# The attention mask of a 192-step transformer pipeline: from a TensorE matmul to a ScalarE copy into PSUM, with two results moved to other banks

## What is computed

```python
qkv = x @ Wqkv                       # 16 heads of 64
q, k = l2norm(q) * qs, l2norm(k) * ksc   # then rotary
sim = einsum('bhwie,bhwje->bhwij', bq, bk2) * 8.0
sim = where(mask, -finfo.max, sim)   # windows of 32, own and previous
out = einsum('bhwij,bhwje->bhwie', softmax(sim), bv2)
x = out.reshape(b, n, 1024) @ Wo + x
```

## Time and profile before

| | us |
|---|---|
| median of 3 runs | 3785.27 |
| lowest, highest run | 3783.42, 3791.43 |
| the profiled execution | 3787.83 |
| its span | 3786.0 |

### The profile page before, as it was taken

How to read it: one execution, slowest core, us unless ns; L and a number is a source line. 1 busy time by engine, 2 the same in 40 slices (tenths; PEclk the granted TensorE clock), 3 DMA queues, 4 the chain that set the end, 5 groups by cost and what they waited for, 6 DMA issues and landing times.

```text
span 3786.0 us, 101581 instructions
## 1 busy us (share of the span) xinstructions
PE 3558.4 (94%) x42643; PEld 2250.6 (59%) x42643; DVE 3058.2 (81%) x5670; ACT 2037.8 (54%) x3871; POOL 2086.7 (55%) x1217
## 2 busy tenths in 40 slices
PE   8999699999999999999999999999999999999997
PEld 4555366666665666666665666666656666566664
DVE  3443698888898888888888898888888888888884
ACT  2222356565565565565655655656556556556553
POOL 0000376666566666666665666666666666666662
PEclk9999899999999999999999999999999999999998
DMA  2000000000001000001000001000001000000000
GB/s 66 1 1 1 7 10 12 28 10 10 9 14 32 10 10 7 10 16 29 10 10 10 7 16 32 10 7 10 10 15 31 10 10 7 14 12 16 10 10 12
DMA packets 62283, 52.55 MB, mean 14 GB/s; under 512 B 11526, under 2 KB 59396, under 8 KB 61828
## 3 DMA queue, kind: packets, MB, share of 16 engines
q1 hardware_dynamic: 61828, 46.05, 4.6%
HBM read 43.93 MB, written 2.10 MB: 12 GB/s over the span
## 4 chain that ended last, share of the span: by engine, by line
PE 62%; DVE 19%; issue 11%; POOL 5%; ACT 2%; DVEq 0%; DMA 0%; SPq 0%; POOLq 0%; ACTq 0%
PE ps L502 16%; PE ps L597 12%; PE ps L657 7%; PE ps L469 6%; PE ps L509 6%; DVE sinp L848 4%; DVE mx L938 3%; PE ps L643 3%; PE ps L551 3%; DVE pT L921 3%; PE ps L485 3%; PE ps L537 3%; POOL cosp L424 2%; POOL cosp L414 2%; DVE ss L854 2%
## 5 line engine op out<-in xcount | busy, mean ns | idle before, releaser
L414 POOL TENSOR_TENSOR cosp<-cosp,rr 128x1024 f32<-128x1024 f32 x384 | 722.5, 1902 | 823.1 <-DVE rr L65 823.0
L424 POOL TENSOR_TENSOR cosp<-cosp,sinp 128x1024 f32<-128x1024 f32 x384 | 904.7, 2368 | 96.1 <-DVE sinp L848 95.5
L502 PE MATMUL ps<-w_qk,xs 128*128 128x512 f32 x1536 | 814.9, 656 | 19.8 <-ACT sq L709 14.2
L597 PEld LDWEIGHTS ps<-px,w_vo 128*128 128x128 f32 x6144 | 729.5, 197 | 155.2 <-issue 118.7
L597 PE MATMUL ps<-px,w_vo 128*128 128x128 f32 x6144 | 739.6, 280 | 22.9 <-issue 18.4
L709 ACT ACTIVATE sq<-ps 128x1024 f32<-128x1024 f32 x384 | 393.1, 1024 | 571.3 <-DVE sinp L848 571.3
L845 DVE TENSOR_TENSOR cosp<-ps,tab 128x1024 f32<-128x1024 f32 x384 | 469.6, 1223 | 267.6 <-PE ps L502 267.4
L749 ACT COPY px<-ps 128x512 f32<-128x512 f32 x768 | 398.8, 598 | 431.0 <-PE ps L657 428.2
L657 PE MATMUL ps<-pT,xtm 32*128 32x512 f32 x3072 | 539.6, 629 | 88.3 <-DVE hh L869 74.7
L502 PEld LDWEIGHTS ps<-w_qk,xs 128*128 128x128 f32 x1536 | 279.9, 203 | 403.5 <-issue 401.8
L854 DVE TENSOR_REDUCE ss<-sq 128x16 f32<-128x1024 f32 x384 | 455.6, 1187 | 60.9 <-ACT sq L709 60.5
(11 more groups left out here) (101 smaller groups left out, 4094.2 us busy)
## 6 DMA issues: line engine op xcount, KB each, us to landing
tab<-in_tab SPq DMA_DIRECT2D x96, 128.0 KB, 2.0
qks<-in_scales SPq DMA_DIRECT2D x96, 128.0 KB, 3.2
w_qk<-in_L_ffn_Wqkv SPq DMA_DIRECT2D x12, 512.0 KB, 6.9
w_v<-in_wv_t SPq DMA_DIRECT2D x6, 512.0 KB, 8.7
w_o<-in_L_ffn_Wo SPq DMA_DIRECT2D x6, 512.0 KB, 9.1
x<-in_L_attn_x SPq DMA_DIRECT2D x16, 128.0 KB, 3.4
out<-w_v SPq DMA_DIRECT2D x16, 128.0 KB, 2.4
w<-in_L_ffn_W SPq DMA_DIRECT2D x6, 341.0 KB
```

The source lines that it names most:

```text
L414: eng.tensor_tensor(v, v, rr[:, B % 2, HEADS * i:HEADS * i + HEADS].unsqueeze(2).to_broadcast([P, HEADS, DH]), ALU.mult).then_inc(rot_read ...
L424: eng.tensor_tensor(cosp[:, A % 2, i, :], cosp[:, A % 2, i, :], sinp[:, i, :], ALU.add).then_inc(rot_added, 1)
L502: t = eng.matmul(ps[:, u, :], xs[:, n % ROUND, :], w_qk[:, n // TILES % 2, i, 512 * u:512 * u + 512], start=True, stop=True)
L597: t = eng.matmul(S0, w_vo[:, i // HP, i % HP, :], px[:, i, :], start=i == 0, stop=i == HEADS - 1)
```

## The change

- The mask is no longer written by TensorE, except for the first tile. In each step ScalarE copies the bf16 mask table into S (both banks, 128x1024) between its `xtm` and `qT` copies; it waits there for `centered` of the tile before and signals `mask_written`, for which the scores wait. The scores are added to what the copy left.
- The output projection goes to `Y`, the start of G(3) (bank 7), and the transposed tokens go to `X`, the start of G(0) (bank 4). The wait for `centered` ahead of the output projection goes.
- G(3) and G(0) are also the banks of the turned keys and of two of the Wv-Wo products. So the waits for `y_added` and `xt_evac` of the same step now stand ahead of `turn(B, 1)`, and in the layer step ahead of L608 too (L609 in the new numbering).

```diff
-        S0 = ps[:, 2, 0:P]
-        S1 = ps[:, 3, 0:P]
         G = lambda k: ps[:, 4 + k, :]
+        Y = G(3)[:, 0:P]
+        X = G(0)[:, 0:P]
@@ TensorE, step
-                if tile(C):
-                    eng.wait_ge(centered, C + 1)
                 if tile(E):
                     eng.wait_ge(px_evac, 4 * (E + 1))
...
-                        t = eng.matmul(S0, w_vo[:, i // HP, i % HP, :], px[:, i, :], start=i == 0, stop=i == HEADS - 1)
+                        t = eng.matmul(Y, w_vo[:, i // HP, i % HP, :], px[:, i, :], start=i == 0, stop=i == HEADS - 1)
...
-                    eng.transpose(S1, xs[:, C % ROUND, :], ident[:, :]).then_inc(xt_done, 1)
+                    eng.transpose(X, xs[:, C % ROUND, :], ident[:, :]).then_inc(xt_done, 1)
                 L = layer_of(s)
                 if L is not None:
                     eng.wait_ge(wv_in, 16 * (L + 1))
                     eng.wait_ge(wo_in, 16 * (L + 1))
+                    after(eng, y_added, E + 1)
+                    eng.wait_ge(xt_evac, C + 1)
...
                     project(A, 1)
+                if tile(E):
+                    eng.wait_ge(y_added, E + 1)
+                if tile(C):
+                    eng.wait_ge(xt_evac, C + 1)
                 if tile(B):
                     eng.wait_ge(rot_ready, 2 * B + 2)
                     turn(B, 1, K_BANKS)
...
                 if tile(B):
-                    if tile(E):
-                        eng.wait_ge(y_added, E + 1)
-                    after(eng, xt_evac, B)
-                    w = window(B)
-                    for h2 in range(2):
-                        eng.matmul(ps[:, 2 + h2, :].rearrange("p (h k) -> p h k", k=DH), ident_bf[:, :],
-                                   mask[:, DH * w:DH * w + DH].unsqueeze(1).to_broadcast([P, HP, DH]), start=True, stop=False, skip_group_check=True)
+                    if B == 0:
+                        for h2 in range(2):
+                            eng.matmul(ps[:, 2 + h2, :].rearrange("p (h k) -> p h k", k=DH), ident_bf[:, :],
+                                       mask[:, 0:DH].unsqueeze(1).to_broadcast([P, HP, DH]), start=True, stop=False, skip_group_check=True)
+                    after(eng, mask_written, B)
                     eng.wait_ge(turn_evac, 4 * B + 4)
@@ ScalarE, step
-                    eng.copy(xtm[:, C % NG, C % ROUND // 2, :], S1).then_inc(xt_evac, 1)
+                    eng.copy(xtm[:, C % NG, C % ROUND // 2, :], X).then_inc(xt_evac, 1)
+                if tile(B) and B:
+                    w = window(B)
+                    eng.wait_ge(centered, B)
+                    eng.copy(S, mask[:, DH * w:DH * w + DH].unsqueeze(1).to_broadcast([P, HEADS, DH])).then_inc(mask_written, 1)
```

More of the change, by code:

```diff
@@ L224, in build @@
         turn_evac = sem("turn_evac")
+        mask_written = sem("mask_written")
         sims_done = sem("sims_done")
@@ L646, in step @@
                 if tile(C):
-                    eng.wait_ge(xt_evac, C + 1)
                     eng.wait_ge(p_turned, C + 1)
@@ L913, in step @@
                     eng.wait_ge(y_done, E + 1)
-                    eng.tensor_tensor(xb[:, batches(E), tile_cols(E)], S0.rearrange("p (b t) -> p b t", b=GB),
+                    eng.tensor_tensor(xb[:, batches(E), tile_cols(E)], Y.rearrange("p (b t) -> p b t", b=GB),
                                       xa[:, batches(E), tile_cols(E)], ALU.add).then_inc(y_added, 1)
```

## The result

| | before | after |
|---|---|---|
| median, us | 3785.3 | 3834.2 |
| lowest, highest | 3783.4, 3791.4 | 3832.5, 3836.1 |
| profiled execution's span | 3786.0 | 3832.5 |

The changed kernel is slower: ratio 1.0127, 95% interval 1.0109 to 1.0144, 49 us. The forecast had the sign, and the range held the time, but it said 17 us.

What follows compares the result with a forecast made beforehand. It took TensorE and VectorE to hand the pace to each other, with a 5.55 us floor in the first half-step. -6 + 11 + 12 = +17 us on 3787.8 gave 3805, or 3802 us on the median's footing; range 3778 to 3850.

Steps and rivals of the forecast that it cites:

- What bounds the kernel: Each step: first half has a 5.55 us floor with engines in series; VectorE works through the second half in order.
- TensorE is the bound: Whole kernel: TensorE sets the pace and gives back its mask time, 99 us less, 3697 us; chance 0.06.
- The mask's removal gives 6 us in kind 2: Chain from kind-1 scores to kind-2 keys: scores 0.52 us earlier gain 0.14 us in 42 steps, -6 us.
- The copy costs nothing: ScalarE's mask copy ahead of `qT`: 1.02 us, covered by TensorE's 1.44 us of idle before `kT`, cost 0.
- The moved waits ahead of the keys' transposes cost nothing: Ahead of the keys' transposes: `y_added` ends 0.3 us before they start, so the moved waits cost 0.
- The layer steps, +11: L608 in layer steps must wait for `y_added`: 2.1 us in five steps, 0.6 in the first, +11 us.
- The clock, +12: Kind 0: TensorE's wait for VectorE's last `glu` grows to about 2.2 us; with layer steps, more clock falls, +12 us.
- rival 3: Every round: clock falls for longer, starting before the low-density L657 passes; 3871 us, half of it 3830; chance 0.12.
- Rival 2: Whole kernel: the clock does not care, or falls less, 3774 to 3791 us; chance 0.27.

Runs made afterwards that it cites:

- the second copy: Changed kernel with VectorE's last kind-0 `glu` moved earlier, and ScalarE copying the mask twice in each step: 3695.5 us, against 3675.3 with one copy.
- the filler runs: Matmuls nobody reads put in TensorE's kind-0 wait: seven in the kernel before, 3704.2 us; in the changed kernel nine, 3737.5 us, or seven, 3726.2 us.
- The same edit ahead of the stand: Changed kernel with the mask matmuls back on TensorE ahead of the scores: in every step 3801.9 us, in kind-0 steps only 3787.0 us.

## Why the prediction was right or wrong

- *What bounds the kernel*: right. 382 fewer matmuls gave no time outside kind 2, and VectorE's idle time grew. The rival "TensorE is the bound" would have given 3697.
- *The mask's removal gives 6 us in kind 2*: right. Kind 2 went from 16.53 to 16.38 us at full clock, 39 times, 5.5 us in sum.
- *The copy costs nothing*: right, with the forecast duration and cover; the second copy shows how much cover there is.
- *The moved waits ahead of the keys' transposes cost nothing*: right. Kind 3 differs by 0.1 us in 44 steps.
- *The layer steps, +11*: right in mechanism. 22.27 against 19.99 is 2.3 each, and 0.7 for the first, 12.1 us; the falls in two of them are another 5.2, where I had counted 4 in the clock's term.
- *The clock, +12*: **this step failed, by size**. It measured some 38 us: 33 in kinds 0 and 1, 5 in the layer steps. I counted only spared rounds that would fall once, five of them at 1.6 us. In fact full clock was left in 2 rounds and not 10, and eleven more rounds than before fell for long, at 3.3. By the prices of the earlier trace rows that is (27 x 3.3 + 16 x 1.6) - (16 x 3.3 + 19 x 1.6) = 31.5 us, against the 33.1 of kinds 0 and 1. The price was right, the count was not. The cause that I gave was right only in part: the stand was to grow to 2.2 us and grew to 1.79, so the length of the stand that I went by does not carry the count. And the falls behind the kind-3 steps, 2.7 of the 33 us, I had at nothing: I took those steps for safe because they were at their floor. That falls would also start earlier and last longer I had as rival 3 at 0.12, with a full effect of 81; what came is half of it, and forecast and rival should not have been kept as either-or. How much of the size is the pattern's own scatter is open: kernels with the same timing of the kind-0 step differ by 27 to 44 us of half-clock time in kinds 0 and 1 (130, 147 and 174 us with the mask matmuls; 212 and 239 without).
- *Rival 2*, the clock does not care: 3774 to 3791 was not it; the filler runs show what the clock does cost, 83 us in the kernel before.
- The Trainium skill (TensorE: Matmul & The Clock Gate, "A second HAM failure mode: psum-queue depth-cycling") says that small idle gaps between groups of matmuls make the clock fall and recover. These traces agree, for gaps of 1.6 to 1.8 us in kind 0, which went with a fall in 27 to 43 of 45 stretches; gaps of 1.0 us did little (3 of 45).

What stays open: why the exact pattern of falls shifts as it does, and what in the shorter work ahead of the stand brings more of them. The same edit ahead of the stand gave 3802 and 3787 us, and the runs of one of these kernels lay up to 28 us apart (one more, of 5530 us, is not counted).

## What to carry to other kernels

Before taking matmuls away from TensorE, find the stand that follows them and ask what clock comes after it: time that was filled and cheap may turn into idle time behind which more rounds run at half clock. Follow every kind of step, also those whose own length does not change: the fall can be paid for in the next one. The larger gain is to remove the stand itself, by looking for the one instruction it waits for and what was put ahead of it on its engine: one `glu` moved ahead of two other instructions gave 130 us, twenty times what the whole mask edit could. And a result moved to another bank brings its reader's wait along, into every other use of that bank, the rare ones too.

## What the runs showed of the hardware that was not expected

- The same idle time of about 2.0 us in a step, as 1.00 and 1.01 with 2.5 us of matmuls between, left 42 of 45 stretches at full clock; as 0.29 and 1.79 it left 2 of 45.
- A fall late in a kind-3 step, 3.4 us of half clock, costs that step at most 0.2 us and the first half of the next one 0.4 to 1.2 us.
- Seven bf16 matmuls of 128x512, 1.68 us in each round in which nothing useful is computed, keep the clock up and save 83 us in 48 rounds.
- ScalarE's copy of 128x1024 from bf16 in SBUF to fp32 in PSUM took 1032 ns, the same as its square from PSUM to SBUF (1024 ns).
